# Taking the identity products out of the six steady rounds of a decoder block on one core

## What is computed

```
x = x + attn(layernorm(x))            # gated delta rule, 16 heads of 16: a state of 16x16 per head and batch row
x = x + xattn(layernorm(x), ctx)      # differential cross attention to 64 context rows, two softmaxes per head
x = x + ffn(layernorm(x))             # conv + silu, router top 2 of 8 experts, RMS norm, gelu feed-forward of 64
```

## Time and profile before

| | |
|---|---|
| median of 3 runs | 1631.13 us (1631.0 to 1631.2) |
| the profiled execution: its own time, its span | 1631.66 us, 1629.9 us |
| PE busy (share of the span) | 1526.6 us (94%) |
| DVE busy | 1220.2 us (75%) |
| ACT busy | 845.6 us (52%) |
| GpSimd (POOL) busy | 204.8 us (13%) |
| granted TensorE clock, mean | 0.985 of full speed |

### The profile page before, as it was taken

The page is one execution under the profiler, slowest core; times in us unless marked ns, Lnnn a source line. Parts: engine busy times, 40 slices in busy tenths (PEclk is TensorE's granted clock), DMA queues, the critical chain, the costliest instruction groups (busy, mean ns, idle before and its releaser), DMA issues.

```text
span 1629.9 us, 39565 instructions
## 1 busy us (share of the span) xinstructions
PE 1526.6 (94%) x16532; PEld 1040.2 (64%) x16598; DVE 1220.2 (75%) x3201; ACT 845.6 (52%) x1612; POOL 204.8 (13%) x212
## 2 busy tenths in 40 slices
PE   5899899999999999999999999999999999999888
PEld 3475677656766577656765577656766577757665
DVE  6256868886788878886798877877798867875553
ACT  1354454655646474655646474655646474534333
POOL 0030212011300112011300112011200112010000
PEclk7999989999999999999999999999999999999999
DMA  5010001000100001000100001000100001000000
GB/s 228 1 27 27 3 1 28 27 2 14 28 6 23 2 14 27 28 2 15 27 13 16 2 15 27 27 2 4 38 1 15 2 14 28 15 2 14 1 1 13
DMA packets 20217, 31.75 MB, mean 19 GB/s; under 512 B 1480, under 2 KB 17864, under 8 KB 19784
## 3 DMA queue, kind: packets, MB, share of 16 engines
q1 hardware_dynamic: 20040, 29.22, 6.2%
HBM read 20.81 MB, written 8.39 MB: 18 GB/s over the span
## 4 chain that ended last, share of the span: by engine, by line
PE 77%; DVE 17%; ACT 3%; issue 3%; DVEq 0%
PE bank L1781 15%; PE bank L1518 7%; PE bank L1729 6%; PE bank L1397 6%; PE four L1590 4%; PE bank L1440 4%; PE bank L1719 4%; PE bank L1520 3%; PE bank L1422 3%; PE bank L1705 3%; PE four L1642 2%; PE four L1609 2%; PE four L1658 2%; PE bank L1429 2%; PE four L1422 2%
## 5 line engine op out<-in xcount | busy, mean ns | idle before, releaser
L1781 PE MATMUL bank<-w_sb,cs 128*128 128x512 f32 x512 | 257.8, 614 | 0.1
L791 ACT ACTIVATE cs<-bank 128x512 f32<-128x512 f32 x128 | 76.2, 595 | 203.5 <-remote 130.3
L510 POOL TENSOR_TENSOR decayed<-state,pk 128x512 f32<-128x512 f32 x64 | 69.7, 1090 | 716.4 <-DVE state L1165 716.4
L1440 PE MATMUL bank<-c_sb 128*128 128x128 f32 x1070 | 141.1, 286 | 5.3 <-DMA c_sb<-in_consts 5.3
L1440 PEld LDWEIGHTS bank<-c_sb 128*128 128x128 f32 x1070 | 134.4, 200 | 17.7 <-issue 10.9
L1729 PE MATMUL bank<-vx_sb,cs 128*128 128x136 f32 x1024 | 136.7, 286 | 8.1 <-ACT cs L745 8.1
L745 ACT COPY cs<-bank 128x512 f32<-128x512 f32 x128 | 74.9, 585 | 127.0 <-PE bank L1719 127.0
L1345 DVE SCALAR_TENSOR_TENSOR cs<-cs,rwt 128x256 f32<-128x256 f32 x224 | 117.9, 526 | 26.9 <-ACT cs L791 14.8
L1729 PEld LDWEIGHTS bank<-vx_sb,cs 128*128 128x128 f32 x1024 | 125.7, 192 | 17.0 <-ACT cs L745 11.6
L1781 PEld LDWEIGHTS bank<-w_sb,cs 128*128 128x128 f32 x512 | 89.5, 189 | 73.0 <-issue 64.1
L1518 PE MATMUL bank<-hT,w_sb 128*128 128x512 f32 x256 | 124.4, 608 | 9.1 <-ACT pre L595 6.2
(11 more groups left out here) (243 smaller groups left out, 2990.5 us busy)
## 6 DMA issues: line engine op xcount, KB each, us to landing
xt<-in_x SPq DMA_DIRECT2D x8, 512.0 KB, 4.8
vscr<-qkv SPq DMA_DIRECT2D x8, 512.0 KB, 2.6
vT<-vscr SPq DMA_DIRECT2D x32, 128.0 KB, 4.4
Tm<-in_x SPq DMA_DIRECT2D x8, 512.0 KB, 3.8
out<-cs SPq DMA_DIRECT2D x8, 512.0 KB, 2.9
w_sb<-in_weights SPq DMA_DIRECT2D x1, 3656.0 KB, 19.1
w_sb<-in_weights SPq DMA_DIRECT2D x1, 1840.0 KB, 9.1
cs<-in_scratch SPq DMA_DIRECT2D x3, 256.0 KB, 9.5
```

The lines of the kernel that those rows point to most:

```text
L1440: mm(bank[7 if i > 0 else 6][:, 0:P], ident, ident, start=True, stop=True)
L1781: mm(dst, x1T[:, k, b * TB:b * TB + TB], ew[:, k, ep * 512:ep * 512 + 512], start=k == 0, stop=False)
```

## The change

One line of the `KEEP` table loses its four entries of class 1, and nothing else is changed:

```diff
-        (0, 0, "co", 5, 0): 20, (0, 0, "co", 6, 0): 4, (0, 0, "onorm", 0): 2, (0, 0, "vturn"): 28, (1, -1,
-        "ffu", 0): 4, (1, -1, "ffu", 1): 11, (1, -1, "pt", 13): 2, (1, 0, "sum", 0): 8, (NI - 1, -1, "pt", 13):
+        (0, 0, "co", 5, 0): 20, (0, 0, "co", 6, 0): 4, (0, 0, "onorm", 0): 2, (0, 0, "vturn"): 28, (NI - 1, -1, "pt", 13):
```

## The result

The changed kernel takes 1657.49 us (median of 4 runs, 1656.02 to 1658.80) against 1631.16 for the kernel before: ratio 1.0158, 95% interval 1.0142 to 1.0174. It is slower, as forecast, but by 26 us where 8.4 were forecast, and lies outside the stated range. The profiled execution took 1658.25 us, its span is 1656.5.

What follows compares the result with a forecast made beforehand. TensorE, busy 94% of the span, was the engine to look at, with the products in its waits; 1631.66 - 1.2 + 9.6 = 1640.1 us for the profiled execution, 1639.5 us as median, range 1629.0 to 1646.9.

Steps and rivals of the forecast that it cites:

- The products lie in waits: All four groups: TensorE waits there anyway; only `ffu.1` starts 0.2 us sooner a round, -1.2 us in all.
- the products were on the path: Rival at the round's end: each round gains 3.54 us and the clock holds, 1609.9 us; chance 0.03.
- the bounds given: Gain ahead of `ffu.1`: 0 to 0.35 us a round, 0 to -2.1 us in all.
- The gaps: TensorE idle ahead of `ffu.1` for 2.8 us and ahead of `sum.0` for 2.45 us once the products are gone.
- One fall at each round's end: From `ffu.1` or in `wo.1`: the clock drops to half speed once in each of six rounds, 6 x 1.6 = +9.6 us.
- the upper price of 1.7: Round's end: half of a 3.4 us stretch lost to one fall of the clock, 1.7 us at most.
- How often: Number of added clock falls in steady rounds: cases 0, 6 or 12; six taken, one a round end.
- two falls a round: Rival: falls at the round's end and behind `pt.13` or at `sum.0`, 12 x 1.6 = 19.2 us, 1649.1 us; chance 0.15.
- The price of a fall: Any steady round: one clock fall costs 1.6 us, read from whole rounds with and without one, difference 1.56 us.
- busy some 25 us less: Sign in the next profile: TensorE's busy time drops some 25 us and yet the span is longer.
- Whole rounds of some 184.5 us or more, none of 183: Sign in the next profile: every steady round has this length because of the clock fall at its end.

Runs made afterwards that it cites:

- e8: Kernel before with 10 products in place of 11 ahead of `ffu.1`, 3 for 2 ahead of `pt.13`, 10 for 8 ahead of `sum.0`: 1632.81 us, ratio 0.9996.
- e10: Kernel before with 10 products in place of 11 ahead of `ffu.1`, all else the same: 1635.14 us, ratio 1.0006.
- e12: Kernel before with 10 products in place of 11 ahead of `ffu.1` and 4 in place of 2 ahead of `pt.13`: 1630.35 us, ratio 0.9975.
- e1: Kernel before with 23 of the 25 products out, the 2 ahead of `pt.13` kept: 1640.84 us, ratio 1.0054.
- e5: Kernel before with only the 11 products ahead of `ffu.1` out: 1639.81 us, ratio 1.0040.
- e4: Kernel before with only the 2 products ahead of `pt.13` out: 1646.78 us, ratio 1.0103.
- e6: Kernel before with only the 8 products ahead of `sum.0` out: 1634.94 us, ratio 1.0018.
- e2: Kernel before with only the 11 products ahead of `ffu.1` kept, the other three groups out: 1654.94 us, ratio 1.0149.
- e3: Kernel before with the 4 products ahead of `ffu.0` and the 8 ahead of `sum.0` out: 1636.34 us, ratio 1.0023.
- e11: Kernel before with the 2 products ahead of `pt.13` out and `pv.6` moved ahead of `db` on TensorE: 1659.57 us, ratio 1.0166.

## Why the prediction was wrong, point by point

- **The products lie in waits: right.** `ffu.1` follows `gelu.1` at once (594.05 + 0.47 = 594.52, matmul at 594.58), and `gelu.1` itself came no sooner: it starts 3.91 us behind the end of its table load (588.86 + 1.28 = 590.14), as before. So the rival "the products were on the path" falls. The gain was put at 0.2 us a round; undisturbed rounds with 10 in place of 11 (e8, e10, e12) take 182.8 us in place of 183.0. With all 25 out `ffu.1` starts 0.29 us sooner, 7.76 us behind `turn6.1` (586.82) in place of 8.05 (577.99 before), as ScalarE's end reaches the matmul in 0.06 us where 0.15 were taken. That makes -1.2 us to -1.7 us, inside the bounds given.
- **The gaps: right.** 2.62 and 2.29 us of idle time, forecast as 2.8 and 2.45.
- **One fall at each round's end, 1.6 us each, +9.6: right.** `ffu.1` to the start of `x1` took 590.57 - 586.04 = 4.53 us before and 600.89 - 594.58 = 6.31 after, 1.78 us more, a little above the upper price of 1.7. Less the 0.29 us this is 1.49 us net a round, where 1.6 less 0.2 were forecast; e1 and e5, which have this fall alone, have rounds of 184.4 to 184.65.
- **"How often", the step that failed.** The text took one fall a round and set the stretch behind `pt.13` aside as the rival "two falls a round", chance 0.15. It fell in all six rounds. The text had seen that taking the 2 products out makes this stretch thinner in every round, and yet the sum had no term for it. e4 takes out these 2 alone and the stretch falls in four of six rounds; e1 puts them back and it falls in none.
- **The price of a fall was taken as one number.** For the rival it gave 12 x 1.6 = 19.2 us and 1649.1. Behind `pt.13` the fall costs 187.80 - 182.97 - (1.78 - 0.29) = 3.34 us a round, and e4's first steady round, which has this fall alone, gives the same 3.3. The 1.56 us of the earlier trace rows had been read from one fall there with the products in place and one at the router. Without them the clock stays down for 6.8 us, and in three of e4's rounds for 10.
- **TensorE "busy some 25 us less": wrong.** It was busy for 5.7 us more, since the records in a low stretch take up to twice as long (`wo.1` 4.75 us for 3.62, a group of `db`'s L1529 1.04 us for 0.53). "Whole rounds of some 184.5 us or more, none of 183" came true, but with 187.8.
- The sum with what was measured: six rounds at 1.49 at the end and 3.34 behind `pt.13` are 29.0 us; three of before's rounds had falls of their own, 1.66 + 1.45 + 1.48 = 4.6 us, and 1.2 us of the last end's loss lies behind the seventh `wo.1`'s start, which leaves the 23.2 us that the rounds show. The 2.4 us ahead of the first `wo.1` have no instruction of the change in them. The forecast had the sign right and 1.4 of the 4.83 us a round; the rest was in the rival, and there at less than half its price.
- **The Trainium skill's page "TensorE: Matmul & The Clock Gate", seeing it yourself:** its example of a clock that comes down 5.2 us after the last matmul does not carry over. Here it fell 3.0 us after the last matmul (591.96 to 595.0), with TensorE at work again for 0.4 us, and behind `pt.13` with TensorE busy for 2.43 of 3.4 us.

Open: why the clock comes down in one round and not in the next with the same instructions (e6, e10), why a fall behind `pt.13` lasts longer without the 2 products even where most of `db` is through, and whether the 4 products ahead of `ffu.0` do anything. The falls also repeat: once a round has one, in most profiles all later rounds have it at the same place. That was seen, not explained.

## What to carry to other kernels

Work that no one waits for can be worth more than work on the path: 2 products of 0.23 us in a 0.77 us wait saved some 16 us in e1. Before such filler is removed, look for each place what runs in the few microseconds behind it: here a fall cost about half of the time that the clock was down (1.78 us of 3.4, 3.3 of 6.8, 4.95 of 10), and how long it was down differed by place and by cover, so a price must be read from a fall in that stretch without the cover. And cover the waits one by one: with one gap filled, the next took the fall (e2, e3).

## What the runs showed of the hardware that was not expected

- Rounds settle to the same length: 187.8 us to within 0.1 us in after, in e2 and in e11, although the falls lie at other places in each, and 184.4 us in most rounds with one short fall, be it in `wo.1`, at `sum.0` or behind `pt.13`.
- A busy TensorE did not bring the clock back at once: it stayed at 0.50 through the 32-column products of `db` from 670.1 to 673.5, with TensorE busy all the time, and through the 16 records of `pv.6` with 136 columns, and was up from 677.0 on.
- The kernel before spreads over 1628 to 1642 us. Where its falls come is part of that: the mean granted clock of its runs above 1637.5 us is 0.977 to 0.981, of those below 1628.5 us 0.986 or 0.987.
